# Feed-forward layer norms on token-major tiles, turned a step early and normalised by GpSimd; inverse norms in nine operations

## What is computed

```
for i in range(6):
    x = attn_layer(shift_tokens(x), ...) + x           # q, k: l2norm * scale, rotary; windows of 32
    x = ffn_layer(shift_tokens(x), ...) + x

def ffn_layer(x, g, bln, W1, b1, W2, b2):
    mu = x.mean(-1, keepdims=True)
    var = ((x - mu) ** 2).mean(-1, keepdims=True)
    xn = (x - mu) / jnp.sqrt(var + 1e-05) * g + bln
    hg = xn @ W1 + b1
    a, gate = jnp.split(hg, 2, -1)
    return a * jax.nn.gelu(gate, approximate=False) @ W2 + b2
```

## Time and profile before

| | |
|---|---|
| median of 3 runs (2240.44 to 2240.59) | 2240.58 us |
| profiled execution, its own time | 2238.25 us |
| its span, first to last instruction | 2236.4 us |
| busy: TensorE, VectorE, ScalarE, GpSimd | 2112.3, 1782.4, 1689.7, 1338.1 us |
| 0 to 263 us: first attention and the first turns' lead | TensorE busy 223.8 of 263 |
| 263 to 1767 us: the turns of the first network | TensorE busy 1470.4 of 1504 |
| 1767 to 1898 us: two-way attention | TensorE busy 101.9 of 131 |
| 1898 to 2190 us: second network | TensorE busy 280.3 of 292 |
| 2190 to 2236 us: end | TensorE busy 36.0 of 46 |

### The profile page before, as it was taken

The page is one execution under the profiler, slowest core; times in us unless marked ns, Lnnn a source line. Parts: engine busy times, 40 slices in busy tenths (PEclk is TensorE's granted clock), DMA queues, the critical chain, the costliest instruction groups (busy, mean ns, idle before and its releaser), DMA issues. The chain is left out here.

```text
span 2236.4 us, 90319 instructions
## 1 busy us (share of the span) xinstructions
PE 2112.3 (94%) x33790; PEld 1450.0 (65%) x33790; DVE 1782.4 (80%) x5019; ACT 1689.7 (76%) x5850; POOL 1338.1 (60%) x1270
## 2 busy tenths in 40 slices
PE   7987999999999999999999999999999887899997
PEld 4654766666666666666666666666666664666665
DVE  5986888888888888888888888888887577888874
ACT  4765888877888888888888788878878444788784
POOL 1335776666676667667676666766666125666660
PEclk9998999999999999999999999999999998999999
DMA  4001221122211122112211122211221100000000
GB/s 115 5 3 27 72 60 49 40 55 63 61 43 48 49 67 59 41 44 69 58 50 40 47 71 60 49 42 45 57 54 43 40 15 7 12 14 16 14 9 28
DMA packets 144807, 97.06 MB, mean 43 GB/s; under 512 B 61976, under 2 KB 137408, under 8 KB 144384
## 3 DMA queue, kind: packets, MB, share of 16 engines
q1 hardware_dynamic: 143232, 91.02, 16.1%
q10 hardware_dynamic: 1152, 0.26, 0.1%
HBM read 23.11 MB, written 1.05 MB: 11 GB/s over the span
## 5 line engine op out<-in xcount | busy, mean ns | idle before, releaser
L1938 POOL TENSOR_TENSOR arena<-arena,rnorm 128x512 f32<-128x512 f32 x448 | 455.2, 1044 | 396.6 <-DVE rnorm L2203 395.3
L711 PE MATMUL bank<-wqkv,hs 128*128 128x512 f32 x1344 | 660.8, 611 | 5.0 <-ACT arena L1556 2.5
L1931 POOL TENSOR_TENSOR arena<-arena 128x512 f32<-128x512 f32 x448 | 565.1, 1272 | 66.2 <-DVE arena L2136 66.2
L1585 ACT ACTIVATE arena<-bank,amx 128x64 f32<-128x64 f32 x1536 | 458.6, 336 | 4.7 <-DVE amx L2218 4.5
L1585 ACT ACTIVATION_READ_ACCUMULATOR arena<-bank,amx 128x1 f32 x1536 | 351.9, 229 | 0.0
L711 PEld LDWEIGHTS bank<-wqkv,hs 128*128 128x128 f32 x1344 | 229.5, 191 | 181.0 <-issue 159.9
L1562 ACT ACTIVATE arena<-bank 128x512 f32<-128x512 f32 x426 | 249.2, 617 | 122.2 <-PE bank L732 121.0
L732 PEld LDWEIGHTS bank<-ident,arena 128*128 128x128 f32 x1792 | 212.4, 143 | 196.1 <-issue 154.1
L2131 DVE TENSOR_TENSOR arena<-bank,rot 128x512 f32<-128x512 f32 x448 | 306.5, 684 | 35.0 <-PE bank L711 30.4
L2136 DVE TENSOR_TENSOR arena<-bank,rot 128x256 f32<-128x256 f32 x896 | 333.0, 412 | 0.0
L732 PE MATMUL bank<-ident,arena 128*128 128x128 f32 x1792 | 258.9, 277 | 47.2 <-issue 17.8
(11 more groups left out here) (214 smaller groups left out, 3252.4 us busy)
## 6 DMA issues: line engine op xcount, KB each, us to landing
arena<-arena SPq DMA_DIRECT2D x768, 64.0 KB
wqkv<-in_L_ffn_Wqkv_dram SPq DMA_DIRECT2D x24, 256.0 KB, 3.3
hs<-z SPq DMA_DIRECT2D x128, 32.0 KB, 1.8
hs<-z SPq DMA_DIRECT2D x128, 31.8 KB, 1.9
fx<-z SPq DMA_DIRECT2D x31, 128.0 KB, 2.2
fx<-z SPq DMA_DIRECT2D x31, 127.0 KB, 2.5
wqkv<-in_L_ffn_Wqkv_dram SPq DMA_DIRECT2D x24, 128.0 KB, 2.6
w<-in_L_ffn_W_dram SPq DMA_DIRECT2D x6, 341.0 KB
```

The costliest lines, as they stand in the source:

```text
L711: nc.tensor.matmul(bank[o][:], src[:], wqkv[w][:, off:off + 512], start=True, stop=True).then_inc(AT[name] if part < 2 else AT[name][i], 1)
L1585: ins = nc.scalar.activation(pb[i][0][p % 2][:, h * DH:(h + 1) * DH], bank[3 + g][:, j * DH:(j + 1) * DH], ACT.Exp, bias=amx[p % 2][:, i, ...
L1931: nc.gpsimd.tensor_tensor(t, t, rs[i][c], ALU.add).then_inc(AT["ak" if c else "aq"][i], 1)
L1938: nc.gpsimd.tensor_tensor(t, t, rnorm[p % 2][:, i, HU * c:HU * c + HU].unsqueeze(2).to_broadcast([P, HU, DH]), ALU.mult).then_inc(AT["mk" ...
```

## The change

**Layer norm of the first network.** `fx` is turned to token-major with four transposes (`ff_tokens`, L862 of the new program) as the last thing of the step before A, and ScalarE copies them to SBUF (`ftok`, the tile of `fcen`). VectorE takes mean and variance from there with `bn_stats` and `bn_aggr` in A's first slot, and makes the inverse deviation in its third slot. GpSimd subtracts the mean and multiplies with the inverse deviation, in place, as the last of A (`ff_normalise`). TensorE turns the result back in B (`ff_channels`), and ScalarE's affine reads it from PSUM. Gone are `ff_mean`, `ff_var`, `ff_broadcast`, the centring, the square and VectorE's normalising; the second network keeps them. SP's load of `fx` waits for the previous group's transposes instead of its centring.

**Inverse norms.** `inverse_root` has nine operations instead of eleven (one step of higher order and one Newton step), for `newton`, `ff_newton` and `half_newton`. Their scratch is in SBUF, so `ff_done` and `normal_free` are gone, and all nine of `newton` stand in their own step (in the second network operations 6 to 8 stand in the next).

```
         fx_f = fx[:].rearrange("p b t -> p (b t)")
         ss = sb("ss", [P, 2, 2 * HU])
-        ny = [sb(f"ny{i}", [P, 2, 2 * HU]) for i in range(3)]
+        ny = [sb(f"ny{i}", [P, 2, 2 * HU]) for i in range(2)]
+        n_s, n_b, n_c = (sb(f"n_{n}", [P, 2, 2 * HU])[:] for n in "sbc")
         rnorm = [sb(f"rnorm{i}", [P, 2, 2 * HU]) for i in range(2)]
         amx = [sb(f"amx{i}", [P, 2, HU]) for i in range(2)]
         asum = [sb(f"asum{i}", [P, 2, HU]) for i in range(2)]
         ainv = [sb(f"ainv{i}", [P, 2, HU]) for i in range(2)]
-        fy = [sb(f"fy{i}", [P, 4]) for i in range(4)]
+        fy = [sb(f"fy{i}", [P, 4]) for i in range(3)]
+        f_st = sb("f_st", [P, 4, 6])
+        f_mv = sb("f_mv", [P, 4, 2])
+        f_s, f_b, f_c = (sb(f"f_{n}", [P, 4])[:] for n in "sbc")
         y_mx = sb("y_mx", [P, 4])
         y_sum = sb("y_sum", [P, 4])
...
+        def group_in(s):
+
+            g, rest = divmod(s - 6, 4)
+            return g if rest == 0 and 0 <= g < 24 else -1
...
+
+        def inverse_root(k, s_, b_, c_, y0, y1, last):
+
+            if k == 1:
+                return nc.vector.tensor_scalar(y0.bitcast(I32), s_.bitcast(I32), -0.5, MAGIC, ALU.mult, ALU.add)
+            if k in (2, 6):
+                return nc.vector.tensor_tensor(b_, y0 if k == 2 else y1, s_, ALU.mult)
+            if k == 3:
+                return nc.vector.tensor_tensor(c_, b_, y0, ALU.mult)
+            if k == 4:
+                return nc.vector.scalar_tensor_tensor(out=b_, in0=c_, scalar=P1, in1=c_, op0=ALU.add, op1=ALU.mult)
+            if k == 5:
+                return nc.vector.scalar_tensor_tensor(out=y1, in0=b_, scalar=P0, in1=y0, op0=ALU.add, op1=ALU.mult)
+            if k == 7:
+                return nc.vector.scalar_tensor_tensor(out=c_, in0=b_, scalar=-0.5 * P2 ** 3, in1=y1, op0=ALU.mult, op1=ALU.mult)
+            return nc.vector.scalar_tensor_tensor(out=last, in0=c_, scalar=1.5 * P2, in1=y1, op0=ALU.add, op1=ALU.mult)
...
-                at(sp, FF["cen"], f)
+                at(sp, FF["in"] if ph["net"] == 0 else FF["tok"], f)
...
-                def normal_free(s):
-
-                    at(pe, nt, RSQ * min(s, hi))
-
-                def ff_mean(f, s):
-                    normal_free(s)
+                def ff_tokens(f):
+                    if f == 0:
+                        pe.wait_ge(LN["xn"], NBLK + 4)
                     at(pe, FF["hid"], 3 * f)
                     pe.wait_ge(FF["x"], 32 * (f + 1))
-                    nc.tensor.matmul(bank[2][:], mean_w[:], fx_f, start=True, stop=True).then_inc(FF["mean"], 1)
+                    for j in range(4):
+                        mm = nc.tensor.transpose(bank4[2][:, j, :], fx[:, j, :], ident[:])
+                    mm.then_inc(FF["in"], 1)
+
+                def ff_channels(f):
+                    at(pe, FF["z"], f)
+                    pe.wait_ge(FF["xn"], 2 * f + 2)
+                    for j in range(4):
+                        mm = nc.tensor.transpose(bank4[2][:, j, :], ftok[:, j, :], ident[:])
+                    mm.then_inc(FF["bc"], 1)
...
                     c, f, before = ff_phase(ph, s)
-                    if c == 0 and f >= 0 and slot_ == 0:
-                        ff_mean(f, s)
                     if c == 0 and before >= 0 and slot_ == 1:
                         ff_down(before, s)
-                    if c == 0 and f >= 0 and slot_ == 2:
-                        ff_var(f)
                     if c == 1 and f >= 0 and slot_ == 0:
-                        ff_broadcast(f, s)
-                    if c == 1 and f >= 0 and slot_ > 0:
+                        ff_channels(f)
+                    if group_in(s) >= 0 and slot_ == 3:
+                        ff_tokens(group_in(s))
+                    if c == 1 and f >= 0 and slot_ in (1, 2):
...
+                    feed_forward_0(s, 3)
...
+                def ff_tokens(f):
+                    act.wait_ge(FF["in"], f + 1)
+                    at(act, FF["bc"], f)
+                    nc.scalar.activation(fcen, bank[2][:], ACT.Copy).then_inc(FF["tok"], 1)
...
                 def ff_affine(f):
                     if f % 4 == 0:
                         act.wait_ge(ld_ff, 192 * (f // 4 + 1))
-                    act.wait_ge(FF["xn"], f + 1)
+                    if ni == 0:
+                        act.wait_ge(FF["bc"], f + 1)
+                    else:
+                        act.wait_ge(FF["xn"], f + 25)
                     w = f // 4 % 2
-                    nc.scalar.activation(fxn, fxn, ACT.Identity, scale=lnp[w][:, 0:1], bias=lnp[w][:, 1:2]
+                    nc.scalar.activation(fxn, bank[2][:] if ni == 0 else fxn, ACT.Identity, scale=lnp[w][:, 0:1], bias=lnp[w][:, 1:2]
                                          ).then_inc(FF["aff"], 1)
...
                     if s in (1, 3, 5):
                         g_square(act, (s + 1) // 2, (s + 1) // 2)
-                    if c == 0 and f >= 0:
-                        ff_square(f)
...
+                    if group_in(s) >= 0:
+                        ff_tokens(group_in(s))
...
+                def ff_normalise(f):
+
+                    pool.wait_ge(FF["rstd"], NSQ * (f + 1))
+                    nc.gpsimd.tensor_tensor(ftok, ftok, f_mv[:, :, 0].unsqueeze(2).to_broadcast([P, 4, P]), ALU.subtract
+                                            ).then_inc(FF["xn"], 1)
+                    pool.wait_ge(FF["xn"], 2 * f + 1)
+                    nc.gpsimd.tensor_tensor(ftok, ftok, fy[2][:].unsqueeze(2).to_broadcast([P, 4, P]), ALU.mult
+                                            ).then_inc(FF["xn"], 1)
...
                         divide_all(1, s - 2)
+                    c, f, before = ff_phase(ph, s)
+                    if c == 0 and f >= 0:
+                        ff_normalise(f)
...
+                if s == 1:
+                    ff0_normalise(23)
...
-                def ff_done(s):
-
-                    c, f, before = ff_phase(ph, s)
-                    if f < 0 or c < 0:
...
-                n_s, n_b, n_c = (bank[2][:, 64 + 32 * k:96 + 32 * k].rearrange("p (i n) -> p i n", i=2) for k in range(3))
-
                 def newton(p, first, last):
...
                         if k == 0:
-                            ff_done(p)
-                            if p == 0:
-                                dve.wait_ge(X0["ex2"], NB)
                             dve.wait_ge(AT["ssq"], un(1, p))
                             dve.wait_ge(AT["ssk"], un(1, p))
                             ins = nc.vector.tensor_scalar(n_s, ss[:], 1e-24, None, ALU.max)
                         else:
-                            dve.wait_ge(nt, RSQ * p + k)
...
+                            dve.wait_ge(nt, NSQ * p + k)
+                            if k == NSQ - 1:
+                                for i in range(2):
+                                    at(dve, AT["mq"][i], p - 1)
+                                    at(dve, AT["mk"][i], p - 1)
+                            ins = inverse_root(k, n_s, n_b, n_c, ny[0][:], ny[1][:], rnorm[p % 2][:])
                         ins.then_inc(nt, 1)
...
                     nc.vector.tensor_tensor(x, bank4[7][:, 0, :], x, ALU.add).then_inc(AT["res"][i], 1)
 
+                def ff_stats(f):
+                    dve.wait_ge(FF["tok"], f + 1)
+                    for j in range(4):
+                        ins = nc.vector.bn_stats(f_st[:, j, :], ftok[:, j, :])
+                    ins.then_inc(FF["st"], 1)
+
+                def ff_aggregate(f):
+                    dve.wait_ge(FF["st"], f + 1)
+                    for j in range(4):
+                        ins = nc.vector.bn_aggr(f_mv[:, j, :], f_st[:, j, :])
...
+                            dve.wait_ge(FF["rstd"], NSQ * f + k)
+                            ins = inverse_root(k, f_s, f_b, f_c, fy[0][:], fy[1][:], fy[2][:])
+                        ins.then_inc(FF["rstd"], 1)
...
                     if c == 0 and f >= 0 and slot_ == 0:
-                        ff_centre(f)
+                        ff_stats(f)
+                        ff_aggregate(f)
                     if c == 0 and before >= 0 and slot_ == 1:
                         ff_close(before)
                     if c == 0 and f >= 0 and slot_ == 2:
                         ff_newton(f)
-                    if c == 1 and f >= 0 and slot_ == 0:
...
 
                 def step_0(s):
-                    if live(s - 1):
-                        newton(s - 1, 9, 11)
```

More of the change, by code:

```diff
@@ L29 @@
 RSQ = 11
+NSQ = 9
+P0, P1, P2 = 4.997384728560895, -3.334408639284136, 0.3755197794197683
 NLAYER = 8
@@ L174, in build @@
         ln_rsqrt = sem("ln_rsqrt")
-        FF = {n: sem("ff_" + n) for n in "x mean cen sq var rstd bc xn aff up ge gelu hid y z outer".split()}
+        FF = {n: sem("ff_" + n) for n in "x in tok st mv rstd bc xn aff up ge gelu hid y z outer".split()}
         XP = {n: sem("xp_" + n) for n in "p act dve".split()}
@@ L885, in group_norm @@
                     if s % 2 == 1 and slot_ == 0:
-                        normal_free(s)
```

(28 more changed lines are left out.)

120 lines of the change are left out of this document (31 added, 89 removed).

## The result

The change made the kernel slower: 2256.6 us (median of 4, 2254.5 to 2261.1) against 2240.5 us on the same chip, ratio 1.0079 (95% interval 1.0064 to 1.0094), which is +16.1 us where +6.4 was forecast. The profiled execution took 2261.07 us, 4.5 over its median, with a span of 2259.3; the one before took 2.3 less than its median. So the two traces differ by 22.9 us, and about 7 of that are the executions'.

A forecast was written before the change was run, and what follows sets the result against it. TensorE was taken to bound the kernel; turns 1.4, end of the first network 2 and second network 3 sum to +6.4 us, so 2244.7 us for the profiled execution and 2247 for the median, range 2221 to 2262.

The forecast's parts named there:

- The chain that decides: First network's turns, VectorE's closing operation to TensorE's use of GpSimd's product: TensorE on at 9.55 us, before 9.07.
- +0.06 us per turn: Net cost in the first network's turns: chain +0.48 against 0.42 gained before it; 1.4 us in 23 turns.
- What TensorE saves: First network's turns: mean and variances go, one group of transposes comes; 1.23 us less TensorE work per turn.
- The end of the first network: Last group's transposes behind their load, GpSimd's two products exposed: +2 us, bounds -1.2 and +4.6.
- The second network: Nine operations on SBUF scratch there collide with GpSimd: +3 us, bounds -4.5 and +6.
- ScalarE, and the load under the turns: First network's turns: ScalarE's work unchanged, fx load lands 1.8 us before the new transposes; both costed at nothing.
- no collision: Rival: VectorE's operations find gaps between GpSimd's, 24 us gained in the turns, 2217 us; chance 0.23 with part-way cases.
- PSUM's fixed cost: Rival: inverse operations some 0.06 us shorter each in SBUF, 18 us gained, 2229 us; chance 0.04.
- The turn grows by over 0.5 us: Sign in the first network's turns that would show the prediction wrong.
- within 0.3: Sign for the changed profile: the first network's turn stays at 65.6 us within 0.3.

The follow-up runs named there:

- e10: The kernel before with the paddings of TensorE's list jumped over and not executed (max_nops=0); 2222.5 us, ratio 0.9901 to 0.9930.
- e11: The change with the paddings of TensorE's list jumped over and not executed (max_nops=0); 2232.1 us, ratio 0.9949 to 0.9978 to the kernel before.
- e5: The kernel before with the nine-operation inverse alone, scratch left in PSUM except one factor read twice; 2221.6 us, ratio 0.9904 to 0.9952.
- e6: The kernel before with the nine-operation inverse alone, all its scratch in SBUF; 2234.1 us, ratio 0.9961 to 0.9980.
- e9: The change with ff_newton before the closing operation, paddings jumped over, second network's inverse scratch back in PSUM except one factor; 2185.2 us, ratio 0.9733 to 0.9763.
- e1: The change with 17 empty slots fewer in step c=2 and 17 more in c=0; 2242.1 us, ratio 1.0008 to 1.0027 to the kernel before.

## Why the prediction was right, and where it was not

- **The direction and the range** held, the forecast was 9.7 us too low in the medians, and by the traces 16.5 (22.9 against 6.4): turns +5.8, end of the first network +8.3, two-way attention +4.9, second network -0.5, before and behind all these -2.0. That the turns came out longer at all, as forecast, was luck: without the slots they are 3.3 us shorter.
- **The chain that decides** was right in its steps: norms ready at 8.12 us behind the closing operation (forecast 8.2), TensorE on at 9.45 (9.55), its wait 1.43 (1.6), three operations blocked. "+0.06 us per turn" measures -0.14 when the slots are out of the way (e10, e11). The rule of the Trainium skill ("SBUF — State Buffer", section "Who interferes with whom") that was set beside it holds in e5, e6 and e9: the same operation is 0.96 us in SBUF and 0.19 in PSUM. The prediction told it of two SBUF inputs; the operation that was blocked first has one (L248, a `tensor_scalar`), and the section counts `tensor_scalar` among those that can take the shared ports.
- **What TensorE saves** named the prices rightly, and forgot that the list has a fixed length between two places. "TensorE saves 1.23 us" was read from matmuls; the instructions and waits taken out came back as 17 executed slots, +0.50 us a turn, 11 us. That TensorE's own work did shrink by about the forecast shows in e10 and e11: the turn is 0.14 shorter though the wait for GpSimd is 1.22 longer. The prediction would have needed the line behind `ff_down` and a count. The issue idle of 17.8 us in 25 places was in the waits of the profile before, and 9.9 of it in one.
- **The end of the first network**, +2 with bounds -1.2 and +4.6, was mis-sized: +10.3 in the traces of before and after, +8.7 between e10 and e11. TensorE waits 2.57 us for the load (0.88 before) and then 3.57 for GpSimd, where it had waited 0.52 for VectorE:

```profile
1776.27 1.09 PE L862 MATMUL bank<-ident,fx 128*128 128x128 f32 x4 [2.57 <-DMA fx<-z]
...
1790.63 1.09 PE L869 MATMUL bank<-ident,arena 128*128 128x128 f32 x4 [3.57 <-POOL arena L1997]
```

  Together that is 4.7 us more waiting, where the upper bound had 4.6. The rest goes with the clock: over the last turn and the end the granted clock was 0.88 and 0.88 in the change and 0.89 and 0.91 in e11, against 0.97 and 0.96 in the kernel before and 1.00 and 0.96 in e10. It doesn't follow from the waits alone: e1 has the same two (2.63 and 3.57), its clock was 0.97 and 0.92, and it took 95.6 us there, 3.1 more than before, not 10.3. So the waits are worth about what the bounds said, and some 7 us go with a lower clock whose cause stays open.
- **The second network**, +3, measured +2.5 (groups 41.82 and not 41.39), for the reason given. The two-way attention, in which the second network's first steps already run, was not priced apart: +4.9, at a granted clock of 0.93 after 0.94.
- **ScalarE, and the load under the turns**: costed at nothing, and no wait for either came up in the turns.
- **Rivals**: "no collision" fell by the three blocked operations, PSUM's fixed cost by 0.16 and 0.17 us for the same operation in both. "The turn grows by over 0.5 us" did not come true (0.36), but the turn's staying "within 0.3" failed too.

## What to carry to other kernels

Where an engine's list is padded to fixed places, count the slots of the new list before anything else: an edit that removes instructions can lengthen the padding, and executed padding is work. Try to have it jumped over; here that gave 18 to 27 us. Scratch of short VectorE operations that run beside GpSimd belongs in PSUM, here even where this needed waits. And when two engines hand a result back and forth, look for idle time ahead of the chain into which a part can be moved: this one move gave 37 us.

## What the runs showed of the hardware that I had not expected

TensorE's sequencer goes through empty slots at 0.075 us each, and queued matmuls hide some thirty to forty of them (in c = 0, 39 and 41 show no idle and 56 show 0.28 us; in c = 2, 33 show 0.29 and 50 show 1.6 to 1.7). A jump over 33 to 168 of them takes 0.29 us there in the median (2.0 over the 168) and leaves no issue idle in the profile. A wait in the profile behind a group of four transposes is 0.16 us shorter than what it costs. A list that is not held to fixed places showed stalls of 0.3 to 2.2 us with nothing to wait for, at a place that changes from turn to turn.
